# The late attention's key halves made during the last expert tile, and the last store's wait moved to GpSimd

## The chip, the cores and the metric

One core of one Trainium2 chip runs the kernel. The metric is the device time in microseconds of one execution; lower is better. Besides the timed executions there is one profiled execution, whose trace the rows below come from.

## The reference

Two layers over x of shape (4, 1024, 256), each adding an attention and a feed-forward branch to its input. Layer 0 has a causal softmax attention with one head of width 256 and a mixture of 8 experts, two for each token:

```python
xn = _layernorm(x)
x = x + _L0_attn_ref(xn, Wq, Wk, Wv) + _L0_ffn_ref(xn, Wr, br, W1, b1, W2, b2)
xn = _layernorm(x)
x = x + _L1_attn_ref(xn, W_qkv, W_out) + _L1_ffn_ref(xn, W_r, W_k, W_v, mu_r, mu_k)
```

Layer 1 has a linear attention with 16 heads and rotary positions, and a gated feed-forward branch that mixes each token with the one before it.

## The kernel before, in words

The kernel is three blocks of instruction streams, one stream for each engine (SP, GpSimd, PE, ACT, DVE). At the end of a block all engines meet: none starts the next block before the last has arrived.

1. `norm_route_attend` normalises, routes tokens to experts, scatters their rows into a table in DRAM with 64 indirect DMAs of GpSimd (line 314), and does the layer 0 attention of sequences 0 to 2.
2. `experts` runs 29 expert tiles of 512, 256 or 128 rows. Raw weights are loaded into two buffers that alternate, `s.raw` (even tiles) and `raw_odd` (odd tiles). Every fp32 operand is split into a high half (a rounding copy) and a low half (the rest), and a product is three matmuls. The last tile is number 28, an even one: 256 rows in 4 units. In it PE does the four "up" products, then the four "down" products. For each unit ACT applies the Relu (line 1120) and makes the high half `hh` (line 1124), DVE the low half `hl` (line 1192); `down(3)` of PE waits for the fourth `hl`. DVE adds the bias (`add_bias`, line 1180) into `y`, SP stores `y` to the table `expert_out` in DRAM (line 1008) and waits for the store's semaphore before it arrives at the end of the block.
3. `combine_and_layer1` begins with the layer 0 attention of sequence 3, the late attention. Its keys are `s.xnT_last`, in fast memory since block 1. PE turns three weight matrices (12 transposes, line 1427) and then starts the projections of `project` (lines 1462 to 1464), which wait on `kl_ready`. ACT makes the key's high half `kh` in two instructions (line 1717), DVE its low half `kl` in two (line 1903). GpSimd at the same time fetches expert results with 16 indirect DMAs (`gather`, line 120) for sequence 0 of layer 1. The attention has six steps: PE's `scores(a)` end with a masking matmul (line 1499), then DVE takes the row maximum (line 1879), ACT the exponentials (line 1705), PE turns them (line 1513), ACT and DVE split them (lines 1712 and 1885), and PE multiplies with the values. PE issues `scores(0)`, `scores(1)`, the turn of step 0, the last projection, `scores(2)`, the turn of step 1 and so on; ACT does the exponentials of step 1 before it splits step 0. After it come the four sequences of layer 1.

Of the kernel before, what the change touches and what calls it, by code (L numbers as in the profile page):

```python
# [5 lines left out]
F32 = mybir.dt.float32  # L6
F32R = mybir.dt.float32r
# [3 lines left out]
ALU = mybir.AluOpType  # L11
# [4 lines left out]
P = 128  # L16
# [919 lines left out]
def experts(nc, s, W1, W2, b2, W_qkv, W_r, W_k, W_v, dispatched, expert_out):  # L936
# [4 lines left out]
    with ExitStack() as ctx:  # L941
        def sb(name, shape, dt=F32):
            return ctx.enter_context(nc.sbuf_tensor(name, shape, dt))
# [1 line left out]
        def sem(name):  # L945
            return ctx.enter_context(nc.semaphore(name))

        raw = [s.raw, sb("raw_odd", [P, DC * H + HC * D])]
        w1raw = [r[:, 0:DC * H].rearrange("p (c h) -> p c h", c=DC) for r in raw]
        w2raw = [r[:, DC * H:].rearrange("p (k d) -> p k d", k=HC) for r in raw]  # L950
        w1h, w1l = sb("w1h", [P, 2, DC, H], F32R), sb("w1l", [P, 2, DC, H], F32R)
# [9 lines left out]
        w1_loaded = [s.raw_loaded[0], sem("w1_loaded_odd")]  # L961
        w2_loaded = [s.raw_loaded[1], sem("w2_loaded_odd")]
        y_stored = [sem(f"y_stored{u}") for u in range(2)]
        last_stored = sem("last_stored")
        w1_hi, w1_lo, w2_hi, w2_lo = sem("w1_hi"), sem("w1_lo"), sem("w2_hi"), sem("w2_lo")
        rows_turned, xT_hi, xT_lo = sem("rows_turned"), sem("xT_hi"), sem("xT_lo")
        up_mm, relu_done, h_hi, h_lo, down_mm, y_done = (sem(n) for n in (
# [10 lines left out]

        def y_part(part):
            return ps[:, 4 + part % 2, part // 2 * D:(part // 2 + 1) * D]  # L980

        block = ctx.enter_context(nc.Block())

        @block.sync
        def _(sp):
            def load(tile):
                e = tile.expert(sp)
                if not tile.is_first():
                    if tile.lead is None:
                        sp.wait_ge(rows_turned, tile.j - 1)  # L990
                    load_rows_of_tile(sp, s, dispatched, tile.row, tile.size, tile.parity)
                    if tile.lead is None:
                        sp.wait_ge(w1_lo, NQ * (tile.j - 1))
                        sp.wait_ge(w2_lo, NQ * (tile.j - 1))
                    load_weights(sp, s, W1, W2, e, raw[tile.parity],
                                 (w1_loaded[tile.parity], w2_loaded[tile.parity]))
                if tile.lead is None:
                    sp.wait_ge(y_done, tile.j - 1)
                sp.dma_start(b2row[:, tile.parity, :], b2[ds(e, 1), :].rearrange("e d -> (e d)").partition_broadcast(P)
                             ).then_inc(b2_loaded[tile.parity], 16)  # L1000
                if tile.lead == 1:
                    sp.dma_start(s.wqkv, W_qkv.rearrange("(c p) e -> p c e", p=P)).then_inc(s.later_loaded, 16)
                    for n, w in enumerate((W_r, W_k, W_v)):
                        sp.dma_start(s.wraw[:, n], w.rearrange("(c p) e -> p c e", p=P)
                                     ).then_inc(s.later_loaded, 16)
                if tile.is_last():
                    sp.wait_ge(y_done, MT)
                    sp.dma_start(expert_out[ds(tile.row, tile.size), :].rearrange("(s p) d -> p s d", p=P),
                                 y[:, tile.parity, 0:tile.parts]).then_inc(last_stored, 16)
                    sp.wait_ge(last_stored, 16)  # L1010

            expert_tiles(sp, s, load)

# [77 lines left out]
        @block.scalar  # L1091
        def _(act):
            def split(tile, q):

                cols = slice(q * H // NQ, (q + 1) * H // NQ)
                u = tile.parity
                if q == 0:
                    act.wait_ge(w1_loaded[u], 16 * tile.pairs_before + 16)
                act.activation(w1h[:, u, :, cols], w1raw[u][:, :, cols], ACT.Copy).then_inc(w1_hi, 1)

            def turned_hi(tile):
                act.wait_ge(rows_turned, tile.j + 1)
                act.activation(xTh[:, :, 0:tile.size], turned_rows(tile), ACT.Copy).then_inc(xT_hi, 1)

            first = ExpertTile(s, None, 0)
            split(first, 0)
            turned_hi(first)
            for q in range(1, NQ):
                split(first, q)

            def body(tile):
                e = tile.expert(act)
                for w in range(tile.units):
                    at, slot = w % 2, w % 4
                    act.wait_ge(up_mm, tile.unit + w + 1)
                    if not (tile.is_first() and w < 2):
                        act.wait_ge(h_lo, tile.unit + w - 1)
                    for n in range(tile.chunks):
                        cols = slice(n * tile.size, (n + 1) * tile.size)
                        op = act.activation(h32[:, at, cols], ps[:, slot, cols], ACT.Relu,  # L1120
                                            bias=s.b1T[:, ds(e * HC + w * tile.chunks + n, 1)])
                    op.then_inc(relu_done, 1)
                    act.wait_ge(relu_done, tile.unit + w + 1)
                    act.activation(hh[:, slot, 0:tile.width], h32[:, at, 0:tile.width], ACT.Copy).then_inc(h_hi, 1)  # L1124
                    if tile.is_last():
                        continue
                    later = tile.following()
                    if tile.units == 8 and 3 <= w < 7:
                        split(later, w - 3)
                    if tile.units == 4 and 1 <= w < 3:  # L1130
                        split(later, w - 1)
                    if w == tile.units - 1:
                        turned_hi(later)
                        if tile.units == 4:
                            split(later, 2)
                            split(later, 3)

            expert_tiles(act, s, body)

        @block.vector  # L1140
        def _(dve):
# [30 lines left out]
            def add_bias(tile):  # L1172

                dve.wait_ge(down_mm, tile.j + 1)
                dve.wait_ge(b2_loaded[tile.parity], 16 * tile.pairs_before + 16)
                if tile.lead is None:
                    dve.wait_ge(y_stored[tile.parity], 16 * tile.pairs_before)
                for half in range(0, tile.parts, 2):
                    n = min(tile.parts - half, 2)
                    op = V.tensor_tensor(y[:, tile.parity, half:half + n, :],  # L1180
                                         ps[:, 4:4 + n, half // 2 * D:(half // 2 + 1) * D],
                                         b2row[:, tile.parity, :].unsqueeze(1).to_broadcast([P, n, D]), ALU.add)
                op.then_inc(y_done, 1)

            def body(tile):
                big = tile.units == 8
                later = None if tile.is_last() else tile.following()
                for w in range(tile.units):
# [7 lines left out]
                    if tile.kind == 1 and w in (0, 1):  # L1196
                        split2(tile, w + 2)
                    if later is None:
                        continue
                    if big and w >= 4:  # L1200
                        split1(later, w - 4)
# [17 lines left out]
def combine_and_layer1(nc, s, expert_out, W_out, mu_r, mu_k, rope_cos, rope_sin, out):  # L1219
# [8 lines left out]
    with ExitStack() as ctx:  # L1228
# [14 lines left out]
        with ExitStack() as attention_only:  # L1243
# [1 line left out]
                return [attention_only.enter_context(nc.sbuf_tensor(name + half, shape, F32R)) for half in "hl"]  # L1245

            zh, zl = parts("z_last_", [P, DC, T])
            kh, kl = parts("key_last_", [P, DC, T])
            vh, vl = parts("v_last_", [P, BT, D])
            pTh, pTl = parts("pT_last_", [P, 2, BT, P])  # L1250
        xkT, xrT = sb("xkT", [P, DC, T]), sb("xrT", [P, DC, T])
        feat = sb("feat", [P, BT, 2 * D])
        act_k, gate = sb("act_k", [P, DC, T]), sb("gate", [P, BT, D])
        oT, att = sb("oT", [P, DC, T]), sb("att", [P, BT, D])
# [33 lines left out]
        wh_ready, wl_ready, xh_ready, xl_ready = (sem(n) for n in ("wh_ready1", "wl_ready1", "xh_ready1", "xl_ready1"))  # L1288
        out_mm, out_added, final, stored = (sem(n) for n in ("out_mm", "out_added", "final", "stored"))
        gate_added, last_final = sem("gate_added"), sem("last_final")  # L1290
        kh_ready, kl_ready, proj_mm, proj_hi, proj_lo = s.projecting
        score_mm, max_done, prob_ready, prob_turned, pT_hi, pT_lo, pv_mm, inv_done, attended = s.attending

        def x_tile(t, n=1):
# [76 lines left out]
        def _(pool):  # L1371
            def gather_beside(b):
# [3 lines left out]
                for start, size, count in units(b):  # L1376
                    pool.wait_ge(combined, count)
                    for i in range(start, start + size):
                        product, count = beside[i]
                        pool.wait_ge(product, count)  # L1380
                        gather(pool, s, expert_out, b + 1, i)

            gather(pool, s, expert_out, 0, 0)
            pool.memset(same_head[:, :], 1.0).then_inc(const_ready, 1)
            pool.memset(xnT[:, :, 0:1], 0.0).then_inc(const_ready, 1)
# [277 lines left out]
        def _(act):  # L1663
# [48 lines left out]
                act.activation(pTh[:, a % 2, 0:blocks_of(a), :].rearrange("p j q -> p (j q)"), turned_columns(a), ACT.Copy  # L1712
                               ).then_inc(pT_hi, 1)

            for half in range(2):
                at = slice(half * 512, (half + 1) * 512)
                act.activation(kh[:, :, at], s.xnT_last[:, :, at], ACT.Copy).then_inc(kh_ready, 1)
            act.wait_ge(weights_turned, 1)
            act.activation(wT[:, :, :, :].rearrange("p n c d -> p n (c d)"), ps[:, 4:7, :], ACT.Copy
                           ).then_inc(weights_ready, 1)  # L1720
# [91 lines left out]
        def _(dve):  # L1812
# [84 lines left out]
                                                row_inv[:, i:i + 1], x_tile(LAST * BT + i), ALU.mult, ALU.add)  # L1897
                op.then_inc(attended, 1)

            for half in range(2):  # L1900
                at = slice(half * 512, (half + 1) * 512)
                dve.wait_ge(kh_ready, LAST + half + 1)
                V.tensor_tensor(kl[:, :, at], s.xnT_last[:, :, at], kh[:, :, at].bitcast(F32), ALU.subtract
                                ).then_inc(kl_ready, 1)
            project_lo(range(3))
            dve.wait_ge(wh_ready, 1)
            V.tensor_tensor(wqkvl[:, :, :], s.wqkv, wqkvh[:, :, :].bitcast(F32), ALU.subtract).then_inc(wl_ready, 1)
# [131 lines left out]
def build(nc, t, out):  # L2039
# [5 lines left out]
    with ExitStack() as ctx:  # L2045
# [2 lines left out]
        norm_route_attend(nc, s, t["L0_attn_x"], t["L0_attn_Wq"], t["L0_attn_Wk"], t["L0_attn_Wv"],  # L2048
                          t["L0_ffn_Wr"], t["L0_ffn_br"], t["L0_ffn_b1"], t["L0_ffn_W1"], t["L0_ffn_W2"],
                          xn_rows, dispatched)  # L2050
        experts(nc, s, t["L0_ffn_W1"], t["L0_ffn_W2"], t["L0_ffn_b2"], t["L1_attn_W_qkv"], t["L1_ffn_W_r"],
                t["L1_ffn_W_k"], t["L1_ffn_W_v"], dispatched, expert_out)
        combine_and_layer1(nc, s, expert_out, t["L1_attn_W_out"], t["L1_ffn_mu_r"], t["L1_ffn_mu_k"],
# [38 lines left out]
```

## Time and profile before

| | us |
|---|---|
| median of 3 timed executions | 1011.66 (1010.92 to 1011.83) |
| the profiled execution's own time | 1009.63 |
| its span, first to last instruction | 1008.0 |
| PE busy in the span | 885.7 (88%) |
| DVE, ACT, GpSimd busy | 669.9, 538.5, 183.1 |

The profiled execution has 1.63 us around its span. PE is busy for 88% of the span, so what matters is where it is not, and what it waits for there. The border between blocks 2 and 3 lies at about 700 us, and the first steps of the late attention reach to about 732 us.

### The profile page before, as it was taken

What the parts mean: (1) busy time and instruction counts of PE and PEld (TensorE: products, weight loads), DVE (VectorE), ACT (ScalarE), POOL (GpSimd) and SP (SyncE); (2) the same over time, 40 slices, a digit from 0 to 9 for tenths busy, and PEclk for the clock granted to TensorE, in tenths of its full rate; (3) what the DMA queues carried; (4) which work ended last, traced back from release to release, by engine and by line L of the source; (5) the groups of instructions that cost most, each with busy time, mean ns of one, the idle gap of its engine ahead of it and who ended that gap; (6) DMA issues with size and microseconds to landing.
All of it is one profiled execution on the core that took longest, in us unless ns stands there. A gap on an engine that the chain in (4) does not pass through costs nothing. (4 is left out here: it accounts for less than half of the span.)

```text
span 1008.0 us, 16807 instructions
## 1 busy us (share of the span) xinstructions
PE 885.7 (88%) x5871; PEld 799.7 (79%) x5871; DVE 669.9 (66%) x1287; ACT 538.5 (53%) x995; POOL 183.1 (18%) x198
## 2 busy tenths in 40 slices
PE   3898111999899999999999999998889999899898
PEld 3687100888799999999999999998778787878777
DVE  7785000545667678787777878775387779687774
ACT  3632000433655667576576756655457757577681
POOL 1005774000000000000000000001603436053202
PEclk8998555999899999999999999999899999999999
DMA  8762445000833736665474666541300112021101
GB/s 271 266 222 89 156 156 182 1 1 1 273 125 120 234 132 231 199 209 182 169 248 134 211 220 202 191 148 58 85 1 27 58 43 82 4 78 47 42 1 42
DMA packets 92576, 129.54 MB, mean 129 GB/s; under 512 B 8464, under 2 KB 78544, under 8 KB 92528
## 3 DMA queue, kind: packets, MB, share of 16 engines
q1 hardware_dynamic: 83728, 103.08, 31.1%
q0 software_dynamic: 8800, 25.83, 8.2%
q8 instruction: 29, 0.48, 0.2%
q14 instruction: 19, 0.16, 0.1%
HBM read 93.50 MB, written 35.39 MB: 128 GB/s over the span
## 5 line engine op out<-in xcount | busy, mean ns | idle before, releaser
L1120 ACT ACTIVATE h<-ps,b1T 128x512 f32<-128x512 f32 (+2 forms) x232 | 112.8, 517 | 156.2 <-PE ps L1032 156.0
L1030 PE MATMUL ps<-w2h,hh 128*128 128x256 f32 x568 | 162.7, 286 | 0.0
L1032 PE MATMUL ps<-w2h,hl 128*128 128x256 f32 x568 | 160.7, 283 | 0.0
L1031 PE MATMUL ps<-w2l,hh 128*128 128x256 f32 x568 | 160.7, 283 | 0.0
L1030 PE MATMUL ps<-xTh,w1h 128*128 128x512 f32 (+2 forms) x464 | 150.1, 323 | 2.4 <-DVE xTl L1164 2.4
L1031 PE MATMUL ps<-xTl,w1h 128*128 128x512 f32 (+2 forms) x464 | 150.4, 324 | 0.0
L1032 PE MATMUL ps<-xTh,w1l 128*128 128x512 f32 (+2 forms) x464 | 149.6, 322 | 0.0
L1192 DVE TENSOR_TENSOR hl<-h,hh 128x512 fp32r<-128x512 f32 (+1 forms) x160 | 100.8, 630 | 73.0 <-ACT hh L1124 70.9
L1019 POOL DMA_DIRECT2D expert_out<-y x28 | 20.7, 740 | 504.1 <-DVE y L1180 504.1
L1030 PEld LDWEIGHTS ps<-w2h,hh 128*128 128x128 f32 x568 | 108.7, 191 | 1.9
L1031 PEld LDWEIGHTS ps<-w2l,hh 128*128 128x128 f32 x568 | 108.8, 192 | 1.7
L1032 PEld LDWEIGHTS ps<-w2h,hl 128*128 128x128 f32 x568 | 108.7, 191 | 0.0
L1124 ACT ACTIVATE hh<-h 128x512 fp32r<-128x512 f32 (+1 forms) x160 | 93.5, 584 | 5.1
L1030 PEld LDWEIGHTS ps<-xTh,w1h 128*128 128x128 f32 x464 | 89.1, 192 | 8.1 <-DVE xTl L1164 2.6
L1032 PEld LDWEIGHTS ps<-xTh,w1l 128*128 128x128 f32 x464 | 88.9, 192 | 7.5
L1031 PEld LDWEIGHTS ps<-xTl,w1h 128*128 128x128 f32 x464 | 89.1, 192 | 5.0
L120 POOL DMA_INDIRECT raw<-expert_out,slots x64 | 72.8, 1138 | 92.4 <-PE ps L1451 61.3
L314 POOL DMA_INDIRECT dispatched<-rows,slots x64 | 61.6, 963 | 86.1 <-DVE tile_expert L802 66.9
L556 ACT ACTIVATE vh<-ps 128x512 fp32r<-128x512 f32 x12 | 7.1, 597 | 88.9 <-remote 80.2
L1449 PE MATMUL ps<-wqkvh,xh 128*128 128x256 f32 (+1 forms) x128 | 44.1, 345 | 4.0 <-DVE x_acc L1896 2.3
L569 ACT ACTIVATE shared<-ps,neg_max 128x1024 f32<-128x1024 f32 (+7 forms) x24 | 17.7, 740 | 55.9 <-DVE neg_max L808 55.9
L393 PE MATMUL ps<-xh,zh 128*128 128x512 f32 (+3 forms) x72 | 26.3, 365 | 22.7 <-DVE vl L668 22.7
(294 smaller groups left out, 2116.6 us busy)
## 6 DMA issues: line engine op xcount, KB each, us to landing
raw<-in_L_ffn_W SPq DMA_DIRECT2D x30, 1024.0 KB
raw_odd<-in_L_ffn_W SPq DMA_DIRECT2D x28, 1024.0 KB, 7.3
dispatched<-shared SPq DMA_DIRECT2D x1, 9088.0 KB, 32.2
expert_out<-y POOLq DMA_DIRECT2D x11, 512.0 KB, 4.1
rows<-dispatched SPq DMA_DIRECT2D x20, 256.0 KB, 3.7
xn_rows<-raw SPq DMA_DIRECT2D x4, 1024.0 KB, 5.2
rows<-xn_rows SPq DMA_DIRECT2D x32, 128.0 KB
b2row<-in_L_ffn_b SPq DMA_DIRECT2D x29, 128.0 KB, 3.0
```

The source lines that it names most:

```text
L120: pool.indirect_dma_start(out=s.picked_rows[:, i, k, :], out_offset=None, in_=expert_out, in_offset=bass.IndirectOffsetOnAxis(ap=slot, axi ...
L314: pool.indirect_dma_start(out=dispatched, out_offset=bass.IndirectOffsetOnAxis(ap=slot, axis=0), in_=xrow[:, t % 4], in_offset=None).then_ ...
L393: pe.matmul(out, ah, bh, start=start, stop=False, skip_group_check=True)
L569: op = act.activation(prob[:, a % 2, 512 * q:512 * q + L], score_columns(a, q, i), ACT.Exp, bias=neg_max[:, i:i + 1], accum_out=row_sum[:, ...
L1019: pool.dma_start(expert_out[ds(tile.row, tile.size), :].rearrange("(s p) d -> p s d", p=P), y[:, tile.parity, 0:tile.parts]).then_inc(y_st ...
L1030: pe.matmul(out, ah, bh, start=start, stop=False, skip_group_check=True)
L1031: pe.matmul(out, ah, bl, start=False, stop=False, skip_group_check=True)
L1032: return pe.matmul(out, al, bh, start=False, stop=stop, skip_group_check=True)
L1120: op = act.activation(h32[:, at, cols], ps[:, slot, cols], ACT.Relu, bias=s.b1T[:, ds(e * HC + w * tile.chunks + n, 1)])
L1124: act.activation(hh[:, slot, 0:tile.width], h32[:, at, 0:tile.width], ACT.Copy).then_inc(h_hi, 1)
L1192: V.tensor_tensor(hl[:, slot, at], h32[:, slot % 2, at], hh[:, slot, at].bitcast(F32), ALU.subtract).then_inc(h_lo, 1)
L1449: pe.matmul(dst, ah(c), bh(c), start=(c == 0), stop=False)
```

## The change

- The two `kh` instructions (ACT) and the two `kl` instructions (DVE) leave the start of block 3 and are issued in the last expert tile, behind the second and the third unit. `kh` and `kl` now lie where `raw_odd` lay, which the last tile doesn't use; `xkT` and `xrT` get places of their own.
- The last tile's result is written to a free half of `s.rows` instead of `y`, so that it lives beyond block 2.
- SP still stores it, but doesn't wait. GpSimd waits for the store in block 3, ahead of its first gather.

```diff
@@ experts @@
-        raw = [s.raw, sb("raw_odd", [P, DC * H + HC * D])]
+        raw = [s.raw, s.raw_odd]
-        last_stored = sem("last_stored")
+        def y_rows(tile, first, n):
+            return (s.rows[:, 1 - tile.parity, first:first + n] if tile.is_last()
+                    else y[:, tile.parity, first:first + n, :])
...
@@ experts, sync @@
                     sp.dma_start(expert_out[ds(tile.row, tile.size), :].rearrange("(s p) d -> p s d", p=P),
-                                 y[:, tile.parity, 0:tile.parts]).then_inc(last_stored, 16)
-                    sp.wait_ge(last_stored, 16)
+                                 y_rows(tile, 0, tile.parts)).then_inc(s.last_stored, 16)
@@ experts, scalar, behind hh of unit w @@
                     if tile.is_last():
+                        if 1 <= w < 3:
+                            act.activation(kh[:, :, key_half(w - 1)], s.xnT_last[:, :, key_half(w - 1)], ACT.Copy
+                                           ).then_inc(kh_ready, 1)
                         continue
@@ experts, vector, behind hl of unit w and split2(tile, w + 2) @@
                     if later is None:
+                        if w in (1, 2):
+                            dve.wait_ge(kh_ready, s.B - 1 + w)
+                            V.tensor_tensor(kl[:, :, key_half(w - 1)], s.xnT_last[:, :, key_half(w - 1)],
+                                            kh[:, :, key_half(w - 1)].bitcast(F32), ALU.subtract).then_inc(kl_ready, 1)
                         continue
@@ combine_and_layer1, gpsimd @@
+            pool.wait_ge(s.last_stored, 16)
             gather(pool, s, expert_out, 0, 0)
@@ combine_and_layer1, scalar and vector @@
-            for half in range(2):
-                at = slice(half * 512, (half + 1) * 512)
-                act.activation(kh[:, :, at], s.xnT_last[:, :, at], ACT.Copy).then_inc(kh_ready, 1)
...
-            for half in range(2):
-                at = slice(half * 512, (half + 1) * 512)
-                dve.wait_ge(kh_ready, LAST + half + 1)
-                V.tensor_tensor(kl[:, :, at], s.xnT_last[:, :, at], kh[:, :, at].bitcast(F32), ALU.subtract
-                                ).then_inc(kl_ready, 1)
```

## Rows read from the trace of the kernel before

**Rows 1.** The page: the span.
```profile
span 1008.0 us, 16807 instructions
```

**Rows 2.** Timeline of the border: start us, duration us, engine, line, what, count, idle before.
```profile
698.83 0.28 PE L1032 MATMUL ps<-w2h,hl 128*128 128x256 f32 x1
699.14 0.69 DVE L1180 TENSOR_TENSOR y<-ps,b2row 128x512 f32<-128x512 f32 x1 [3.43 <-PE ps L1032]
699.86 0.39 SPq L1008 DMA_DIRECT2D expert_out<-y  x1
...
702.48 2.00 ACT L1717 ACTIVATE key_last_h<-xnT_last 128x1024 fp32r<-128x1024 f32 x2 [7.49 <-PEq L941]
702.49 2.79 PE L1427 MATMUL ps<-ident,shared 128*128 128x128 f32 x12 [3.39 <-PEq L941]
...
703.20 1.03 POOL L120 DMA_INDIRECT raw<-expert_out,slots  x1 [13.53 <-POOLq L941]
703.57 2.36 DVE L1903 TENSOR_TENSOR key_last_l<-xnT_last,key_last_h 128x1024 fp32r<-128x1024 f32 x2 [3.73 <-ACT key_last_h L1717]
...
704.93 0.71 PE L1462 MATMUL ps<-key_last_h,folded 128*128 128x512 f32 x1
...
705.49 0.40 PE L1463 MATMUL ps<-key_last_l,folded 128*128 128x512 f32 x1
```

**Rows 3.** SP's own waits at the border: us in total, times, longest.
```profile
SPq L941 <- DMA expert_out<-y: 1.8, 1, 1.8
```

**Rows 4.** Windows: length, busy us of each engine (instructions), granted clock, DMA share, GB/s.
```profile
252.00:253.40 1.40, 0.00 (x0) 0.00 (x0) 0.88 (x2) 0.13 (x1) 0.00 (x0) 1.00 0.00 0
253.40:254.60 1.20, 1.06 (x8) 0.86 (x8) 0.67 (x1) 0.56 (x2) 0.00 (x0) 1.00 0.00 0
699.00:702.00 3.00, 0.10 (x1) 0.00 (x0) 0.69 (x1) 0.00 (x0) 0.00 (x0) 1.00 0.25 87
702.00:705.00 3.00, 2.51 (x13) 2.54 (x13) 1.44 (x2) 2.00 (x2) 1.50 (x2) 0.51 0.35 89
```

**Rows 5.** Timeline of the last expert tile, units 2 and 3, and down(3).
```profile
692.04 0.84 ACT L1120 ACTIVATE h<-ps,b1T 128x256 f32<-128x256 f32 x2
...
692.91 0.63 ACT L1124 ACTIVATE hh<-h 128x512 fp32r<-128x512 f32 x1
...
693.43 0.69 DVE L1158 TENSOR_TENSOR w2l<-raw,w2h 128x512 fp32r<-128x512 f32 x1
...
695.02 0.69 DVE L1192 TENSOR_TENSOR hl<-h,hh 128x512 fp32r<-128x512 f32 x1 [0.29 <-ACT hh L1124]
...
697.50 0.28 PE L1030 MATMUL ps<-w2h,hh 128*128 128x256 f32 x1
```

**Rows 6.** Timeline of the first steps of the late attention.
```profile
717.73 0.23 PE L1499 MATMUL ps<-above,ident_b 128*128 128x128 bf16 x1
...
720.31 0.23 PE L1499 MATMUL ps<-above,ident_b 128*128 128x128 bf16 x1
...
721.63 1.23 DVE L1879 TENSOR_REDUCE neg_max<-ps 128x1 f32<-128x1024 f32 x1 [4.38 <-PE ps L1499]
...
724.15 1.97 PE L1513 MATMUL ps<-ident,qk 128*128 128x128 f32 x8 [3.61 <-ACT qk L1705]
724.19 0.94 POOL L120 DMA_INDIRECT raw<-expert_out,slots  x1 [0.30 <-issue]
...
727.34 1.09 DVE L1879 TENSOR_REDUCE neg_max<-ps 128x1 f32<-128x896 f32 x1 [4.49 <-remote]
...
731.89 0.96 PE L1513 MATMUL ps<-ident,qk 128*128 128x128 f32 x7 [0.66 <-DVE pT_last_l L1885]
```

**Rows 7.** Timeline of the same handover in sequence 1's attention.
```profile
177.60 0.23 PE L440 MATMUL ps<-above,ident_b 128*128 128x128 bf16 x1
...
177.87 1.22 DVE L808 TENSOR_REDUCE neg_max<-ps 128x1 f32<-128x1024 f32 x1 [1.78 <-PE ps L440]
```

**Rows 8.** A window within the scatters of the first block.
```profile
110.00:160.00 50.00, 5.59 (x15) 4.01 (x14) 0.88 (x2) 0.00 (x0) 37.91 (x40) 0.50 0.46 153
```

More of the change, by code:

```diff
@@ L980, in y_part, with key_half @@
             return ps[:, 4 + part % 2, part // 2 * D:(part // 2 + 1) * D]
+        def y_rows(tile, first, n):
+            return (s.rows[:, 1 - tile.parity, first:first + n] if tile.is_last()
+                    else y[:, tile.parity, first:first + n, :])
+        kh, kl = s.last_keys
+        kh_ready, kl_ready = s.projecting[0:2]
+        def key_half(n):
+            return slice(n * 512, (n + 1) * 512)
         block = ctx.enter_context(nc.Block())
@@ L1179, in add_bias @@
                     n = min(tile.parts - half, 2)
-                    op = V.tensor_tensor(y[:, tile.parity, half:half + n, :],
+                    op = V.tensor_tensor(y_rows(tile, half, n),
                                          ps[:, 4:4 + n, half // 2 * D:(half // 2 + 1) * D],
@@ L1247, in combine_and_layer1 @@
             zh, zl = parts("z_last_", [P, DC, T])
-            kh, kl = parts("key_last_", [P, DC, T])
             vh, vl = parts("v_last_", [P, BT, D])
             pTh, pTl = parts("pT_last_", [P, 2, BT, P])
-        xkT, xrT = sb("xkT", [P, DC, T]), sb("xrT", [P, DC, T])
+        kh, kl = s.last_keys
+        xkT, xrT = s.mixed
         feat = sb("feat", [P, BT, 2 * D])
@@ L1290, in combine_and_layer1 @@
         gate_added, last_final = sem("gate_added"), sem("last_final")
-        kh_ready, kl_ready, proj_mm, proj_hi, proj_lo = s.projecting
+        _, kl_ready, proj_mm, proj_hi, proj_lo = s.projecting
         score_mm, max_done, prob_ready, prob_turned, pT_hi, pT_lo, pv_mm, inv_done, attended = s.attending
@@ L2050, in build @@
                           xn_rows, dispatched)
+        later = ctx.enter_context(ExitStack())
+        with nc.sbuf_tensor("raw_odd", [P, s.DC * s.H + s.HC * s.D], F32) as raw_odd:
+            s.raw_odd = raw_odd
+        with (nc.sbuf_tensor("key_last_h", [P, s.DC, s.T], F32R) as kh,
+              nc.sbuf_tensor("key_last_l", [P, s.DC, s.T], F32R) as kl):
+            s.last_keys = kh, kl
+        s.mixed = [later.enter_context(nc.sbuf_tensor(n, [P, s.DC, s.T], F32)) for n in ("xkT", "xrT")]
+        s.last_stored = later.enter_context(nc.semaphore("last_stored"))
         experts(nc, s, t["L0_ffn_W1"], t["L0_ffn_W2"], t["L0_ffn_b2"], t["L1_attn_W_qkv"], t["L1_ffn_W_r"],
```

## The prediction

> **What bounds the kernel now.** I read the page first: PE, the matrix engine, is busy for most of the span of 1008.0 us [rows 1], so a change at one border can give back only what PE stands idle or runs slow there. Then the timeline around 700 us, where the change lies. The reader is to see three things in it [rows 2]. PE's last matmul of the expert tiles ends at 698.83 + 0.28 = 699.11, and its next instruction starts at 702.49: 3.4 us of nothing. DVE has the result at 699.14 + 0.69 = 699.83, SP issues the store at 699.86 and is through with the issue at 700.25. And then no engine does anything until 702.45 or so. SP's own list of waits names the cause: 1.8 us on the landing of the store [rows 3], so from 700.25 to 702.05; the remaining 0.4 us is the meeting of the engines.
>
> Then the windows of the granted clock [rows 4]: PE is granted 1.00 up to 702 and 0.51, the lower level of 1.2 GHz, from 702 to 705, after the 3.4 us pause. The 12 transposes of line 1427 run in that slow stretch. Last, the timeline of the late attention. The product of step 0 ends at 717.73 + 0.23 = 717.96, but DVE, idle and waiting for it, starts its row maximum at 721.63; that of step 1 ends at 720.54, and DVE starts at 727.34 [rows 6]. In sequence 1 the same handover takes 0.04 us: 177.60 + 0.23 against 177.87 [rows 7]. So PE's results reach the others 3.7 and 6.8 us late in just this stretch, while GpSimd issues its 16 indirect gathers back to back, from 703.20 [rows 2] to 724.19 + 0.94 = 725.13 [rows 6]. This delay matters for the size of the gain.
>
> **The change part by part, against the profiled execution.**
>
> (a) *SP's wait goes.* The border opens 1.8 us earlier [rows 3]. The meeting itself stays, 0.4 us. Bounds: 1.5 us, if SP's arrival costs more right behind an issue; 2.0 us. I take 1.8. By the Trainium skill (DMA: Bandwidth & Descriptors, section on the anatomy of one DMA) a transfer costs about 2.0 us and its bytes at 436 GB/s; for 256 KB that is an estimate of 2.6 us from issue to landing, and the wait removed would be 2.2 us. The row has 2.2 us from issue to landing, 702.05 - 699.86, and the row decides.
>
> (b) *The key halves in the last tile.* Two ACT copies of 1.0 us and two DVE subtracts of 1.2 us [rows 2]. ACT has no gap there: unit 2 is Relu at 692.04 and high half until 692.91 + 0.63 = 693.54 [rows 5], 1.5 us a unit. The first `kh` goes in at 692.04 and ends at 693.04; unit 2 then ends at 694.54, the second `kh` at 695.5, unit 3 at 697.0. DVE is through with the weights at 693.43 + 0.69 = 694.12; then `kl` to 695.3, `hl` of unit 2 to 695.9, `kl` to 697.1, `hl` of unit 3 (0.69) to 697.8, where before it ended at 695.71. PE's `down(3)` started at 697.50 and needs that `hl`; with its weight load ahead of the matmul it now starts at about 697.9. So 0.4 us is exposed, the rest lies under `down(0)` to `down(2)`. Bounds: 0.2 us, if the instructions overlap a little more, and 4.4 us, if all four lay bare. The bias, the store and the border move back by the 0.4 us with it. Writing the result into `s.rows` has the same shape, so no cost.
>
> (c) *The key halves leave block 3.* Before, the first `kl` ended at 703.57 + 1.18 = 704.75 and the projection started at 704.93, just behind the transposes [rows 2]: they were hidden by the slow transposes, and their leaving gives nothing by itself. It does once the transposes are faster (d): with PE back at 702.49 - 1.8 + 0.4 = 701.1 and transposes of 1.3 us the projection could start at 702.4, while a `kl` made in block 3 would be ready at 703.4. So 1.0 us of the sum below hangs on this part.
>
> (d) *The clock.* PE's pause shrinks from 3.4 to 699.5 to 701.1, 1.6 us. At 252.0 to 253.4 us PE stood still as well, 1.4 us at the other border, and the clock stayed at 1.00; the 8 transposes behind it took some 1.06 us, 0.13 each at most [rows 4]. Twelve at that pace are 1.3 to 1.6 us; before it took 704.93 - 702.49 = 2.4 us to get past them [rows 2]. The first projection matmul lasted 0.71 us against 0.40 for the next [rows 2], 0.3 more. Together 1.5 us less. Bounds: 0, if the clock falls all the same, and 1.5.
>
> So PE reaches the projections 1.8 - 0.4 + 1.5 = 2.9 us earlier, and ends the products of steps 0 and 1 at 715.1 and 717.6.
>
> (e) *GpSimd's wait.* What is queued behind it is the whole gather train, and six short constant instructions, wanted only at the end of the attention. The store now lands at 702.05 + 0.4 = 702.45, and the train started 0.75 us behind the border before. It starts between 702.5 (all that is ready) and 703.3; I take 703.1, in effect where it was. The rows gathered are wanted after step 0 at the earliest, so by itself this is worth nothing either way.
>
> (f) *What becomes of the 2.9 us.* The late handovers decide. The train stays in its place while PE's work moves ahead. In the scatter train of the first block PE got 15 matmuls done in 50 us [rows 8], while GpSimd issued 40 scatters: a long train of indirect DMAs does slow PE and what it hands on, and the delay grows with the age of the train: 3.7 us at age 14.8 (717.96), 6.8 us at age 17.3 (720.54). Lower bound: each handover is as late as before, and the gain stays 2.9. Other bound: the delay goes by the age of the train. Then step 0's product ends at age 11.9 and comes perhaps 1 us late (716.1), step 1's at age 14.5 some 3.6 us late (721.2), and step 0's turned rows at about 725.6. ACT and DVE split them in some 2.3 us, and PE can turn step 1 at 727.9, where it did at 731.89 [rows 6]: 4.0 us earlier. I take the middle, 3.4. The Trainium skill (SBUF — State Buffer, section on who interferes with whom) says that DMA never contends with a compute engine. By that rule the delay belongs to PE's own work and the gain would be 2.9; rows 8 speak against it. Behind step 1 all engines hand on to each other with short waits, and every later part moves by the same amount.
>
> Sum: 1009.63 - 3.4 = 1006.2 us for the profiled execution. The median of the runs is 1011.66, 2.0 us above it; the same difference gives 1008.3 us.
>
> **The rivals.**
>
> *The gathers hold it up.* The handover of step 1 at 727.34 comes just 2.2 us after the last gather is issued. If that is no delay of its own length but a release by the end of the train, it stays at 727.1 to 727.4 whatever PE did before. ACT and DVE then split step 0 as late as before, and the gain is 0.3 us, 1011.4 us. For it: the coincidence, and the train that doesn't move. Against it: step 0's handover was through at 721.63, with the train still running.
>
> *The clock falls all the same*, or the last tile costs 1 us more than I worked out: PE comes 1.4 to 1.9 us earlier and no more, 1010.1 us. For it: the pause is 0.2 us longer than the one that left the clock alone. Against it: it is less than half of the one that didn't.
>
> *Slower: the last tile pays for all four instructions.* If ACT and DVE are so tight that `hl` of units 2 and 3 both come too late, PE stops at `down(2)` and `down(3)`. All four bare are 4.4 us; with 1.8 us won at the border, and nothing from the clock since PE then pauses in the tile too, the kernel is 2.6 us slower, 1014.3 us. It turns slower from 1.8 us exposed. Against it: `down(2)` has its `hl` at 695.9, in time by my sum, if only barely.
>
> **How the numbers follow.** Forecast 0.57, gathers 0.20, clock or tile 0.14, slower 0.06, and 0.03 for more than 4.5 us faster. No change can be told from one of 0.2%, 2.0 us, here. Faster: 0.57 + 0.03 = 0.60; same: 0.20 + 0.14 = 0.34; slower 0.06. The range takes in the forecast's upper bound with some spread, 1011.66 - 4.9 = 1006.8, and reaches over the gathers' case to 1011.7. The forecast's own range is 1006.9 to 1009.3.
>
> **What would show it.** In the changed profile: SP's wait on the store is gone, and PE's pause at the border is 1.6 us; the clock stays at 1.00 in the 5 us behind it; the 12 transposes take 1.6 us or less; the last `hl` ends 2.1 us later against the start of the tile and `down(3)` 0.4 us later; GpSimd's first gather starts where it was to within 0.5 us; the row maxima of steps 0 and 1 start 3 to 6 us earlier. The prediction is wrong if the row maximum of step 1 still starts at 727, if the clock falls at the border, or if PE stops within the last tile for more than 1 us.

## The result and the profile after

The changed kernel takes 1004.96 us, median of 7 runs (1003.67 to 1008.12), against 1011.66 us for the kernel before on the same chip: 0.9939 times the time, interval 0.9928 to 0.995. That is 6.7 us less, where 3.4 us were forecast, and below the range. The profiled execution took 1004.03 us, its span 1002.4 us, 5.6 us under the profiled execution before.

To compare the two traces I count from a common event, the start of the last bias add: 699.14 us in the trace before, 700.50 in the one after. Of the 1.36 us between them the last tile accounts for 0.25, as shown below; the other 1.1 us was there before the last tile began, in a stretch that the change does not touch; such a shift is also seen between traces that share that stretch (698.48 us in `before_again` and 700.95 in `before_warm`, below). It is why the two profiled executions differ by 5.6 us and not by 6.7.

**The border.** Timeline of the changed kernel, the rows that answer to [rows 2]:
```profile
700.18 0.28 PE L1041 MATMUL ps<-w2h,hl 128*128 128x256 f32 x1
700.50 0.69 DVE L1192 TENSOR_TENSOR rows<-ps,b2row 128x512 f32<-128x512 f32 x1 [1.79 <-PE ps L1041]
701.21 0.39 SPq L1018 DMA_DIRECT2D expert_out<-rows  x1
702.00 0.38 SPq L1368 DMA_DIRECT2D wout<-in_L_attn_W_out  x1
702.05 1.50 PE L1444 MATMUL ps<-ident,shared 128*128 128x128 f32 x12 [1.59 <-PEq L941]
703.31 0.48 PE L1479 MATMUL ps<-key_last_h,folded 128*128 128x512 f32 x1
...
703.67 1.03 POOL L120 DMA_INDIRECT raw<-expert_out,slots  x1 [12.89 <-DMA expert_out<-rows]
```
SP issues the store at 701.21 and its next transfer at 702.00, with no wait for a landing between. PE is back after 1.59 us, where it was 3.39, and the projections begin 703.31 - 700.50 = 2.81 us behind the bias add, where it was 704.93 - 699.14 = 5.79. GpSimd's first gather, which now waits for the store, starts 3.17 us behind it (before 4.06).

Windows of the changed kernel (length, busy us of PE, weight load, DVE, ACT and GpSimd, granted clock, DMA share, GB/s); the first answers to the last of [rows 4]:
```profile
702.00:705.00 3.00, 2.95 (x19) 2.69 (x20) 0.00 (x0) 1.41 (x2) 1.03 (x1) 1.00 0.63 175
...
764.00:768.00 4.00, 4.00 (x24) 3.47 (x23) 4.00 (x5) 1.70 (x5) 2.22 (x2) 1.00 0.00 0
...
872.00:877.00 5.00, 5.00 (x33) 4.46 (x32) 1.73 (x4) 2.09 (x4) 2.55 (x2) 1.00 0.00 2
```
The clock is 1.00 at the border, where it was 0.51.

**The last tile.** Its key instructions on ACT:
```profile
693.12 1.04 ACT L1136 ACTIVATE key_last_h<-xnT_last 128x1024 fp32r<-128x1024 f32 x1
...
695.46 1.04 ACT L1136 ACTIVATE key_last_h<-xnT_last 128x1024 fp32r<-128x1024 f32 x1
```
and DVE's work up to the last `hl`:
```profile
695.15 1.22 DVE L1213 TENSOR_TENSOR key_last_l<-xnT_last,key_last_h 128x1024 fp32r<-128x1024 f32 x1
696.28 0.69 DVE L1204 TENSOR_TENSOR hl<-h,hh 128x512 fp32r<-128x512 f32 x1
696.89 1.22 DVE L1213 TENSOR_TENSOR key_last_l<-xnT_last,key_last_h 128x1024 fp32r<-128x1024 f32 x1
698.02 0.68 DVE L1204 TENSOR_TENSOR hl<-h,hh 128x512 fp32r<-128x512 f32 x1
```
The last `hl` ends 1.8 us before the bias add, where it ended 3.4 before it [rows 5]. From the tile's first product to the bias add it is 11.96 us, before 11.72: 0.25 us exposed.

**The late attention.** Products of steps 0 and 1, their row maxima, and the handover that is late instead; they answer to [rows 6]:
```profile
716.14 0.23 PE L1516 MATMUL ps<-above,ident_b 128*128 128x128 bf16 x1
...
716.41 1.23 DVE L1893 TENSOR_REDUCE neg_max<-ps 128x1 f32<-128x1024 f32 x1 [1.55 <-issue]
...
718.72 0.23 PE L1516 MATMUL ps<-above,ident_b 128*128 128x128 bf16 x1
...
718.99 1.09 DVE L1893 TENSOR_REDUCE neg_max<-ps 128x1 f32<-128x896 f32 x1 [1.36 <-issue]
...
721.17 0.28 PE L1481 MATMUL ps<-folded,key_last_l 128*128 128x256 f32 x1
...
724.87 0.95 POOL L120 DMA_INDIRECT raw<-expert_out,slots  x1 [0.30 <-issue]
...
728.07 0.60 ACT L1716 ACTIVATE v_last_h<-ps 128x512 fp32r<-128x512 f32 x1 [5.39 <-remote]
```
Both row maxima start 0.04 us behind their products; before they were 3.7 and 6.8 us late. But ACT then waits 5.39 us for the last part of `v_last`, which PE has finished at 721.17 + 0.28 = 721.45 (the profile finds no releaser on this core and calls it remote). The stall has not gone: it has moved to the next handover, and it eats much of the 6.6 and 9.7 us by which the maxima are earlier behind the bias add. It ends 2.25 us after the last gather's issue (724.87 + 0.95 = 725.82); in the kernel before, the row maximum of step 1 starts 2.2 us after the same event. Behind it the kernel is 4.3 us earlier counted from the bias add, 4.05 with the tile's 0.25 taken off.

**Layer 1.** DVE's mixes of the four sequences, first and last, before:
```profile
764.59 2.48 DVE L1941 SCALAR_TENSOR_TENSOR xkT<-xnT,rest_of_mu,xkT 128x1024 f32<-128x1024 f32 x2 [0.42 <-ACT xkT L1690]
...
951.69 2.48 DVE L1941 SCALAR_TENSOR_TENSOR xkT<-xnT,rest_of_mu,xkT 128x1024 f32<-128x1024 f32 x2 [0.67 <-ACT xkT L1690]
```
and after:
```profile
761.63 2.48 DVE L1950 SCALAR_TENSOR_TENSOR xkT<-xnT,rest_of_mu,xkT 128x1024 f32<-128x1024 f32 x2 [0.36 <-ACT xkT L1707]
...
946.11 2.48 DVE L1950 SCALAR_TENSOR_TENSOR xkT<-xnT,rest_of_mu,xkT 128x1024 f32<-128x1024 f32 x2 [0.67 <-ACT xkT L1707]
```
187.10 us before, 184.48 after: 2.6 us less in a stretch that the change does not touch. The windows say where; these are of the kernel before:
```profile
764.00:768.00 4.00, 4.00 (x16) 3.42 (x15) 3.58 (x5) 2.54 (x3) 0.00 (x0) 0.64 0.02 4
...
872.00:877.00 5.00, 3.99 (x19) 3.92 (x20) 3.73 (x11) 1.81 (x4) 0.00 (x0) 0.66 0.00 0
```
Twice the granted clock falls to its lower level for 3.4 us, from 763.5 and from 872.7, in the trace before; in the one after it does not, once it is past a fall at 751.3. Each of the two comes with a pause of PE, the first with the one from 760.9 to 763.1:
```profile
763.14 0.47 PE L1449 MATMUL ps<-wqkvh,xh 128*128 128x512 f32 x1 [2.27 <-DVE x_acc L1896]
```
Between these two traces the gain is thus 4.05 us at the border and in the late attention, and 2.6 us in layer 1, together 6.7.

### The profile page after: what moved, and what is told of

Its sections match the earlier page's. It is cut to its first block and busy times, and to the rows that moved or that the text cites. A ratio compares the mean times of both kernels' runs of the same rounds, so it can differ in the third digit from the quotient of the medians.

```text
span 1002.4 us, 16806 instructions
## 1 busy us (share of the span) xinstructions
PE 882.4 (88%) x5871; PEld 795.7 (79%) x5871; DVE 669.9 (67%) x1287; ACT 538.4 (54%) x995; POOL 183.7 (18%) x198
## 5 line engine op out<-in xcount | busy, mean ns | idle before, releaser
L668 DVE TENSOR_TENSOR vl<-ps,vh 128x512 fp32r<-128x512 f32 x12 | 8.2, 687 | 67.0 <-ACT vh L556 34.9
L393 PEld LDWEIGHTS ps<-xh,zh 128*128 128x128 f32 x72 | 14.5, 202 | 48.3 <-issue 25.1
```

The source lines that it names most:

```text
L393: pe.matmul(out, ah, bh, start=start, stop=False, skip_group_check=True)
```

## The experiments

Kernels of one comparison run on one chip, beside the kernel before; the comparisons below ran on four chips. They turned out to be of two kinds. On two, as on the chip of the result, the kernel before takes 1010.6 to 1011.7 us; on two others it takes 929. I call them the 1010 us and the 929 us kind; whether the difference lies in the chip or in how it was set up, no run tells. Times are medians; milestones are us behind the last bias add. In the kernel before on the 1010 us kind they are: projections 5.79, row maxima of steps 0 and 1 22.49 and 28.2.

**The two halves of the change apart.** `wait_only` has the wait at GpSimd and makes the keys in block 3; `keys_only` is the change with SP's wait put back. In `wait_only` the subtracts on DVE go back in the same way as the copies on ACT.
```diff
# wait_only, against the kernel after
-                        if 1 <= w < 3:
-                            act.activation(kh[:, :, key_half(w - 1)], s.xnT_last[:, :, key_half(w - 1)], ACT.Copy
-                                           ).then_inc(kh_ready, 1)
...
+            for half in range(2):
+                at = slice(half * 512, (half + 1) * 512)
+                act.activation(kh[:, :, at], s.xnT_last[:, :, at], ACT.Copy).then_inc(kh_ready, 1)
...
# keys_only, against the kernel after
+                    sp.wait_ge(s.last_stored, 16)
-            pool.wait_ge(s.last_stored, 16)
```


> The wait for the last store is moved to GpSimd, the key halves stay at the start of the third block. My sum: the border opens 1.8 us earlier with nothing exposed in the last tile, the clock stays at 1.00, but the projections wait for the key's low half, about 1.0 us. PE is then 2.3 us earlier than before at the projections against 2.95 in the changed kernel, and the kernel takes 1.5 to 3 us less than before plus the 1 us from the gathers: 1007 to 1010. Rival, that the gain is all in the wait: as the changed kernel, 1004 to 1006.

> The key halves are made in the last tile, SP waits for the store as before. My sum: 0.3 us exposed in the tile, the pause and the slow clock at the border as before, the projections not earlier, since the slow transposes covered the key halves: 1011.5 to 1012.5, no gain. Rival, that the earlier keys or the new places in memory carry the gain: 1009 or less.

> The changed kernel once more. If the 2.6 us that its trace won behind the late attention (no slow clock near 763 and 872 us) were the chance of one execution, this profile shows such a slow stretch somewhere in layer 1, and the median lies near 1007. If it is systematic, the clock stays up in layer 1 again and the median is 1004 to 1006.

These fell on the 929 us kind (before 928.75). `wait_only`: 927.83, 0.9983 (0.9969 to 0.9996), projections at 3.91. `keys_only`: 929.08, 0.9998 (0.9984 to 1.0012), projections at 5.78. The changed kernel: 924.65, 0.9959 (0.9946 to 0.9971), projections at 2.81. So the wait brings 1.9 us at the projections, and the keys bring 1.1 on top and nothing alone. In none of the three traces is the row maximum of step 0 or 1 late, and the whole change is worth 4.1 us here rather than 6.7. `wait_only` gains 0.9 us, less than the 1.5 to 3 expected.

**Without the long train.** `before_spaced` is the kernel before, with gathers 4 to 7 of each table held until PE has done the score products of steps 0, 1, 2 and 2. (Where an expectation below says "scores 1 to 3" or "steps 1 to 3", it counts them from one.)
```diff
             for i in range(1, BT):
+                if i >= BT // 2:
+                    pool.wait_ge(score_mm, ATTENDED + min(i - 3, 3))
                 gather(pool, s, expert_out, 0, i)
```


> The kernel before, with the gathers of the second half of sequence 0 held until PE has ended the score products of steps 0, 1, 2 and 2. If the back-to-back train delays PE's handovers, the row maxima of steps 0 and 1 start within 0.2 us of the end of their products, the late attention is about 6 us shorter and the kernel takes 1005 to 1007. Rival, that the lateness belongs to PE's own work (the Trainium skill, SBUF - State Buffer, has it that DMA never contends with a compute engine): handovers as late as before, 1011 to 1012.

On the 929 us kind: 929.08, 1.0007 (0.9991 to 1.0022). There was nothing to win: the maxima start 0.04 us behind their products without the train, and in `keys_only` and `wait_only` with it. (The kernel before itself has no trace on this kind.) What this kind does during the first block's scatters is the contrast to [rows 8]. Its window:
```profile
110.00:160.00 50.00, 49.84 (x354) 45.67 (x353) 25.68 (x45) 20.47 (x37) 38.42 (x39) 1.00 0.47 154
```
GpSimd issues 39 scatters in the 50 us, DMA moves 154 GB/s, as there, and PE does 354 matmuls where it did 15. The first expert tile starts at 178 us instead of 253. That is 76 of the 82 us between the kinds.

**The clock alone, and PE's start alone.** Both fell on the 1010 us kind (before 1010.61), with the kernel before once more.
```diff
# before_warm, against the kernel before: PE kept busy at the end of the last tile
+                if tile.is_last():
+                    for _ in range(24):
+                        pe.transpose(ps[:, 0, 0:P], s.ident[:, :], s.ident[:, :])
# after_pe_waits, against the kernel after: PE alone waits for the store in block 3
+            pe.wait_ge(s.last_stored, 16)
```


> The kernel before, one more look. It tells what the kernel before looks like when its whole time is near 929 us: if the 80 us and the late handovers go together, the row maxima of steps 0 and 1 start within 0.2 us of the end of their products, PE is busy all through the scatters, and the border is as in the first profile (PE's pause 3.4 us, projection 5.8 us behind the bias). If the late handovers are PE's own, they are 3.7 and 6.8 us late here too.

> The kernel before with 24 idle transposes of PE behind the last expert tile (about 2.6 us of work, nothing waits for it), while SP waits for the store. If the clock falls for PE's pause, it stays at 1.00 here, and the projections start 1.1 us earlier and run as from full speed, limited by the key's low half: 1 to 1.5 us less than before. Rival, that the slow stretch is not of the pause: unchanged.

> The changed kernel with PE alone waiting for the last store before its transposes; ACT, DVE and SP go on. It gives PE back the pause of 3.4 us and takes the wait's 1.8 us and, if my reading holds, the clock's 1.2 us from the gain: projection 5.3 to 5.8 us behind the bias, time 0 to 0.5 us around before. Rival, that the gain comes of SP, ACT and GpSimd being earlier: 3 to 4 us less than before, as the changed kernel.

`before_again`: 1009.08 in its one execution, maxima at 22.47 and 28.17 and the falls of the clock in layer 1 in the same places (64.6 and 173.8 behind the bias add; 64.3 and 173.6 in the first trace). The starts of the two late maxima repeat to 0.03 us, although PE's product of step 1 came 0.9 us later this time: its delay is 5.84 us where it was 6.80. So it is the moment of the release that repeats, not the delay.

`before_warm`: 1010.75, 1.0003 (0.9992 to 1.0015). Its border:
```profile
704.30 1.50 PE L1430 MATMUL ps<-ident,shared 128*128 128x128 f32 x12 [0.76 <-PEq L941]
...
706.66 0.50 PE L1465 MATMUL ps<-key_last_h,folded 128*128 128x512 f32 x1 [0.86 <-DVE key_last_l L1906]
```
The transposes take 1.50 us as in the changed kernel, but the projections stand 0.86 us on `key_last_l` and begin at 5.70. The clock is worth next to nothing while the key halves are made in block 3: step (c) of the prediction, seen from the other side. I had expected projections 1.1 us earlier and 1 to 1.5 us from it.

`after_pe_waits`: 1004.58, 0.9951 (0.993 to 0.9971). The projections begin at 5.20, nearly as late as before, and still 6.0 us are won. Its products and maxima:
```profile
721.20 0.23 PE L1517 MATMUL ps<-above,ident_b 128*128 128x128 bf16 x1
...
721.47 1.23 DVE L1894 TENSOR_REDUCE neg_max<-ps 128x1 f32<-128x1024 f32 x1 [1.56 <-issue]
...
723.78 0.23 PE L1517 MATMUL ps<-above,ident_b 128*128 128x128 bf16 x1
```
They end 18.9 and 21.5 us behind the bias add, as PE's products do in the kernel before, and yet DVE gets them on time. This was against what I had forecast: I had tied the gain to PE's early start and the delay to the age of the train. PE's products come 3.1 us later than in the changed kernel; what becomes of that is in a later row of the same trace:
```profile
730.29 0.60 ACT L1717 ACTIVATE v_last_h<-ps 128x512 fp32r<-128x512 f32 x1 [2.60 <-remote]
```
The last part of `v_last` is released 27.8 us behind the bias add, in the changed kernel 27.6, and ACT stands 2.60 us for it instead of 5.39. PE's lateness disappears in the stall, and the row maximum of step 2 starts at 30.7 in the one and 30.5 in the other.

**Keys behind the tile.** `keys_late` puts all four key instructions behind unit 3, on DVE in the same way as here on ACT.
```diff
-                        if 1 <= w < 3:
-                            act.activation(kh[:, :, key_half(w - 1)], s.xnT_last[:, :, key_half(w - 1)], ACT.Copy
-                                           ).then_inc(kh_ready, 1)
+                        if w == 3:
+                            for n in range(2):
+                                act.activation(kh[:, :, key_half(n)], s.xnT_last[:, :, key_half(n)], ACT.Copy
+                                               ).then_inc(kh_ready, 1)
```


> The changed kernel with all four key instructions behind the fourth unit of the last tile, where ACT has nothing else and DVE only the bias. The last low half of the tile is then on time again, PE doesn't stop in the tile (0.25 us less), and the key halves are ready at 698.5 by the scale of the first profile, 0.6 us ahead of the bias: 0.2 to 0.3 us less than the changed kernel, projection 2.8 us behind the bias. Rival, that the second low half delays the bias: 0.3 to 0.6 us more than it.

1004.58, 0.9952 (0.9932 to 0.9972). The tile takes 11.72 us again, so nothing is exposed, the projections begin at 2.81, and the last part of `v_last` is released at 27.5. The 0.25 us is too little for its time to show.

**Again, for the other kind.** A first repeat fell on the 929 us kind. `wait_only_2`: 928.22, 0.9989 (0.9975 to 1.0002); `keys_only_2`: 929.43, 1.0011 (0.9994 to 1.0028); `before_spaced_2`: 929.78, 1.0007 (0.9994 to 1.0021); and `keys_late_spaced`, which joins `keys_late` and the spaced gathers: 925.39, 0.9953 (0.9939 to 0.9966). The maxima of steps 0 and 1 are on time in all four. They repeat the first comparison.

> The changed kernel with the four key instructions behind the last tile's unit 3 and gathers 4 to 7 of each table held for scores 1 to 3. On a chip of the 1010 us kind: if the train holds the handovers, those behind the attention come on time too, 1002 us or 2.5 under the changed kernel; if not, 1004.6 like the changed kernel. On a chip of the 929 us kind: 924.6.

The second repeat fell on the 1010 us kind (before 1011.24).

> The wait goes to GpSimd, the key halves stay in block 3. On a chip of the 1010 us kind: theory A (the train's transfers on top of the small loads make the handovers late; moving SP's wait separates them): 1006.5 us, row maxima of steps 0 and 1 on time at about 17.0 and 19.6 us behind the last bias add. Theory B (it is VectorE's and ScalarE's key work in block 3): at most 1.5 us gained, maxima late. Theory C (a release is late whenever it falls later than about 19 us behind the bias add): step 0 on time, step 1 late. On a chip of the 929 us kind: 928.

> The key halves go to the last tile, SP keeps its wait. On a chip of the 1010 us kind: theory A and C: within 1 us of before, maxima of steps 0 and 1 at about 22.5 and 28.2 us behind the bias add. Theory B: 4 us faster, both on time. On a chip of the 929 us kind: as before within 0.7 us.

> The kernel before with gathers 4 to 7 of each table held for the scores of steps 1 to 3. On a chip of the 1010 us kind: if the train makes the handovers late, maxima on time (18.9 and 21.5 us behind the bias add) and 1007 us; if not, 1010.5 and the maxima as before. On a chip of the 929 us kind: no change.

> The changed kernel with the key instructions behind unit 3 and the same gathers held. On a chip of the 1010 us kind: if the train holds the handovers behind the attention, 1002 us; if not, 1004.6. On a chip of the 929 us kind: 925 us.

| kernel | us | ratio (interval) | projections | maxima 0, 1 |
|---|---|---|---|---|
| wait_only_3 | 1010.68 | 0.998 (0.996 to 1.0) | 3.92 | 21.34, 27.75 |
| keys_only_3 | 1011.78 | 0.9999 (0.9981 to 1.0016) | 5.79 | 21.07, 28.15 |
| before_spaced_3 | 1004.78 | 0.9938 (0.9919 to 0.9956) | 5.79 | 18.85, 21.43 |
| keys_late_spaced_2 | 1003.09 | 0.99 (0.9861 to 0.9938) | 2.81 | 15.91, 18.50 |

DVE in `wait_only_3`, with PE's product of step 0 at 717.62:
```profile
717.62 0.23 PE L1509 MATMUL ps<-above,ident_b 128*128 128x128 bf16 x1
...
722.20 1.23 DVE L1889 TENSOR_REDUCE neg_max<-ps 128x1 f32<-128x1024 f32 x1 [3.73 <-PE ps L1509]
...
728.62 1.09 DVE L1889 TENSOR_REDUCE neg_max<-ps 128x1 f32<-128x896 f32 x1 [5.19 <-remote]
```
and in `before_spaced_3`:
```profile
717.06 0.23 PE L1501 MATMUL ps<-above,ident_b 128*128 128x128 bf16 x1
717.32 1.23 DVE L1881 TENSOR_REDUCE neg_max<-ps 128x1 f32<-128x1024 f32 x1 [0.71 <-PE ps L1501]
...
719.91 1.09 DVE L1881 TENSOR_REDUCE neg_max<-ps 128x1 f32<-128x896 f32 x1 [1.36 <-PE ps L1501]
```
Three things follow. First, the train makes the handovers late: with a gap in it (nothing is issued from 16.0 to 19.1 us behind the bias add) every one is on time. `before_spaced_3` was expected to win 4 us and wins 6.5, as much as the whole change and without anything of it. The two do not win it in the same place. `before_spaced_3` is 6.8 us earlier at the first mix of layer 1 and wins nothing behind it; the change is 4.3 earlier there.

Second, the three theories of the expectations fall. A (the wait frees the handovers) and B (the keys do) fall because neither half frees them by itself. C (late is what falls later than 19 us) falls because `wait_only_3` has the product of step 0 ready at 16.98 and is 4.4 us late, and `after_pe_waits` has step 1 at 21.5 and is on time.

Third, the parts do not add: 0.998 and 0.9999 against 0.9939 for both. `keys_late_spaced_2` has the lowest median on this kind, 8.2 us under the kernel before, but from four executions, and its interval overlaps that of `before_spaced_3`; its twin on the other kind is no slower than the changed kernel there.

## Why the prediction was wrong, step by step

**(a) SP's wait, right.** PE's pause went from 3.39 to 1.59 us, 1.8 less as taken. The fit of the Trainium skill (DMA: Bandwidth & Descriptors, section on the anatomy of one DMA) from which 2.6 us was estimated there is for DMAs that GpSimd issues, and this store is SP's; the row's 2.2 us was the one to go by.

**(b) The last tile, right.** 0.25 us is exposed where 0.4 was taken, within the bounds.

**(c) The keys' leaving, right.** `wait_only` starts its projections at 3.91, the changed kernel at 2.81: 1.1 us hang on it, 1.0 was taken, and `keys_only` shows that it gives nothing alone.

**(d) The clock, right.** It stayed at 1.00, and the transposes took 1.50 us. PE reaches the projections 2.98 us earlier behind the bias add, 2.7 with the tile taken off; the sum had 2.9.

**(e) GpSimd's wait, right on the clock of the trace, less so where it counts.** The train started at 703.67 instead of 703.20. But behind the bias add that is 3.17 us instead of 4.06: it moved 0.9 us ahead, of which the forecast's 703.1 had 0.5.

**(f) What becomes of it: the step that failed.** I took 3.4 us, the middle of 2.9 and 4.0. Measured are 4.05 behind the attention, at my other bound, so this term was 0.65 us short. That it came so near is luck, because the rules behind both bounds are wrong. One had each handover as late as before, the other a delay that grows with the train's age. `after_pe_waits` has no delay at an age at which the kernel before had 6.8 us, and `wait_only_3` is late at a younger one.

What the traces show instead is a release that stands at the end of the train. Eight traces of the 1010 us kind have the train unbroken, and in each the last long stall of the first steps ends 1.9 to 2.5 us after the issue of the last gather. In `before`, `before_again`, `before_warm` and `keys_only_3` the row maximum of step 1 starts at 28.15 to 28.20 us behind the bias add, though PE had ended its product anywhere from 21.4 to 23.0. In `wait_only_3` it starts at 27.75. In the changed kernel, `keys_late` and `after_pe_waits`, whose trains also start 0.9 us earlier, it is the last part of `v_last`, at 27.5 to 27.8. What the change won is that other work is left to do at that moment: from the maximum of step 1 it is 6.6 us to that of step 2 (`before`), from `v_last` 2.9 (`after`). With the release 0.6 us earlier that makes the 4.3 us. No run moves the end of the train by itself, so that it is the end which frees the handover is the reading that fits these traces, not a thing tested; that a gap frees it is shown by `before_spaced_3`.

The larger miss is the sentence "every later part moves by the same amount". Layer 1 gave back another 2.6 us between the two traces, a term that the sum did not have at all, and it is what puts the time below the range.

**The 2.6 us.** The two falls of the clock in the trace before cost 1.5 and 1.1 us between neighbouring mixes. On the 1010 us kind both traces of the kernel before have them, and so do `before_warm`, `keys_only_3` and, moved by the earlier attention, `before_spaced_3` (57.5 and 166.7 behind the bias add) and `wait_only_3` (56.4 and 172.5). The changed kernel, `after_pe_waits` and `keys_late` have one fall at 50.8 to 51.0 and none behind it until the last microsecond. But `keys_late_spaced_2` has falls at 46.3, 162.3 and 227.2, and the changed kernel on the 929 us kind at 54.3 and 163.5.

Are they chance? In part. PE's pauses are in every trace, the falls are not: the changed kernel pauses for 1.7 us at 166.4 as the kernel before does at 172.2, and its clock stays. One and the same kernel can have either. From the first to the last mix `keys_only` takes 189.9 us and `keys_only_2` 184.6, `wait_only` 188.7 and `wait_only_2` 185.6, all on the 929 us kind. So one pair of traces does not carry the 2.6 us. The medians carry some of it: the changed kernel, `after_pe_waits` and `keys_late` are 3.8 to 4.4 us earlier behind the attention in their traces, and 6.0 to 6.7 us faster in medians of 7 to 12 executions. Which pause brings a fall, and why the change should move it, is open; no run here set it alone.

**The rivals.** That the gathers hold it up was priced at 0.3 us and given 0.20. Its mechanism, a release by the end of the train, is the one that fits the traces, and in `wait_only_3`, where the maximum of step 1 is again what it holds, the kernel gains 0.6 us. Its price left out that the changed kernel would have got the two maxima and step 0's turned rows through before that moment. That the clock falls all the same, and that the last tile pays for all four instructions, did not happen.

**What stays open** is why both halves together take the delay from the first two maxima and neither does alone. The train's start and PE's timing are each excluded as the whole cause by a run above, and the train is needed for it but does not decide which handover it hits. And no run tells what sets the two kinds of chip apart.

## What to carry to other kernels

A handover that comes microseconds late beside a train of indirect DMAs is a cost of its own: try first to break the train with a wait, before moving anything else. While such a stall stands, work moved ahead of it counts only by what is left to do when it ends. Two edits at one border can be worth little or nothing alone and much together, when each merely uncovers the other's wait (here SP's store, the slow clock and the keys), so cost them in the order in which they end. And the falls of TensorE's clock at its pauses differ between executions, and may differ with the change: keep 1 to 3 us of range for stretches that the change does not touch, and do not read such a difference from one pair of traces.

## What the runs showed of the hardware

Beside a train of indirect DMAs TensorE is slow on some chips and not on others. In the window of 50 us with some 40 scatters it did 15 matmuls on the chip of [rows 8] and 354 on one of the other kind, at 153 and 154 GB/s. All ten traces of the 1010 us kind have 13 to 19 there, all eight of the 929 us kind over 340. The Trainium skill (SBUF — State Buffer, section on who interferes with whom) says that DMA never contends with a compute engine. The 929 us kind agrees with it; on the 1010 us kind something in such a train does hold up the engines, and these runs do not show where.

On the 1010 us kind sixteen gathers back to back delay some of the handovers of PE's results by 2 to 7 us, while PE itself runs on: in the changed kernel ACT stands 5.39 us for a product that PE has ended. With a gap between the first and the second half of each table's gathers no release is late (`before_spaced_3`, `keys_late_spaced_2`), and the gap costs nothing that shows on the 929 us kind (1.0007).
